# Slots, late mixing and prologue order of an attention and FFN block on one Trainium2 core

## The chip, the cores and the metric

One core of a Trainium2 chip runs the whole program. The metric is the device time of one execution in microseconds (us), the median of several runs. Below, TensorE is also called PE, VectorE DVE, ScalarE ACT, GpSimd POOL and SyncE SP, as in the profile's rows.

## The reference

The input x has 8 batch rows of 512 tokens and 256 channels. The output is `x + attention(layernorm(x)) + ffn(layernorm(x))`, in float32:

```python
xn = _layernorm(x, axis=-1)
q, k, v = xn @ Wq, xn @ Wk, xn @ Wv        # 32 query heads, 8 kv heads of 64
q, k = _rope(q, k)
allowed = (j <= i) & (i - j < 128)          # causal, window of 128
attn = softmax(where(allowed, q k^T / 8, -inf))
a = (attn @ v) @ Wo
h = fwht(xn * SU_ug) / SCALE
g = silu(h @ W_gate.T * (Ws[1024:] * SCALE)) * (h @ W_up.T * (Ws[:1024] * SCALE))
f = fwht(g * SU_dp) / SCALE @ W_down.T * (Ws_dp * SCALE)
```

`fwht` is a normalised Walsh-Hadamard transform, linear, so it can be folded into the weights once: the weights of gate and up are multiplied by the Hadamard matrix and by the signs `SU_ug`, and each of their 2048 output columns has a scale.

## The kernel before, in words

Every large product is done in fp32r with operands split in a high part (an ACT copy, rounded) and a low part (DVE: full minus high). Helper `three` (lines 936 to 940) issues three matmuls, high by high, low by high and high by low, and accumulates them in PSUM. A projection of 128 columns for 512 tokens is 2 x 3 = 6 matmuls of 512 columns.

**A batch row ("row")** has an FFN part and an attention part.

- FFN part (PE lines 1130 to 1147): for 8 hidden tiles j, `hidden("gate", j)`, `hidden("up", j)` and `down(j - 2)`. Before tiles 2 and 4 the two projections of a query group go in between. ACT takes silu of the gate (L614), DVE multiplies by up (L836), ACT and DVE split the product (L643, L697). The values v for token tiles 0 and 1 come last. The part ends when DVE adds the sum to `acc` (L891); this row in the trace marks where one batch row's FFN ends.
- Attention part (PE lines 1161 to 1172): 32 steps (8 kv heads x 4 token tiles), two to a unit, in 17 units u = 0 to 16. In a unit PE does `scores(2u)`, `scores(2u+1)` (L1082), `transposes(2u-2)` (L1096), `fill(2u)`, `transposes(2u-1)`, `fill(2u+1)`, and `values_mixed(u-1)` (L1113, L1125). The last unit has no scores. DVE masks the scores and takes their maximum (L851 or L856, then L858), ACT takes the exponentials (L619), POOL divides by the sum (L504), PE transposes, ACT copies the result out (`t_copy`, L629), POOL masks a copy (L512), PE multiplies by the values. ACT copies the output (`o_copy`, L635) and DVE makes its low part (`o_low`, L697), which also gives the PSUM tile TR free: `transposes` of an even step waits for it (`tr_read`). For token tiles 1 to 3, DVE makes `v_mix` (L898, L899, two copies) and POOL `v_step` (L519) from v.

**Slots.** `fill(n)` issues what is put into slot n by hand: a rope projection of the list `ROPE_SLOTS` (first and second half; DVE's `products`, L741, then POOL's `rotate`, L480 and L482), an output projection of `WO_SLOTS` (12 matmuls of 256 columns; DVE adds it to `acc`, `wo_add`, L768), v for tiles 2 and 3 (slots 1 and 3), or the two transposes of the next row's normalised x (`X_SLOT`, L969; ACT `x_high` L567, DVE `x_low`). All of them go through the two PSUM banks of PROJ in turn, in the order of the list USES: use u waits until use u - 2 has been read (`has_read`, line 942). The last output projections of a row, (7, 0) and (7, 1), are issued within the next row's first two hidden tiles (line 1139).

Each engine's instructions run in the order in which its block lists them; a wait holds everything behind it. SP's block issues nearly all loads, with waits of its own.

**Row 0** also splits the query and output weights (`wq_high`, `wq_low`, `wo_high`, `wo_low`): at the slots of WQ_SPLIT_SLOT and WO_SPLIT_SLOT, ACT and DVE do so at the end of a unit (lines 687 to 691 and 925 to 929). The result is saved to DRAM and loaded by later rows.

**The prologue** folds the gate and up weights. SP loads them in two pieces of 1 MB after x has come (line 358) and broadcasts the column scales over partitions (line 360). PE transposes x, projects k and q, and then multiplies 8 tiles of 512 columns by the Hadamard matrix (L1022, 16 matmuls). For each tile DVE reads the product, scales it by sign and column into `folded` (L796), ACT makes the high part from it (L591), DVE the low part (L697). Then come wq(1), the v weights, and hidden tile 0. POOL rotates k first and then does the three butterfly levels of the down weights (L495, L497), which `down_weights` (L1028) needs.

The few lines that order a unit on DVE:

```python
for u in range(UNITS):
    if u: inverse_sum(2 * u - 1)
    if u >= 2: o_low(b, u - 2)
    if u < UNITS - 1: fold(2 * u); fold(2 * u + 1)
    if u < TT - 1: value_mix(u + 1)
    if u < UNITS - 1: inverse_sum(2 * u)
```

## Time and profile before

| | |
|---|---|
| median of 3 runs | 1334.5 us (1334.47 to 1335.08) |
| profiled execution, its own time | 1334.04 us |
| its span, first to last instruction | 1331.5 us |
| granted TensorE clock, mean | 0.993 of full speed |
| busy: PE, DVE, ACT, POOL | 94%, 70%, 56%, 48% |
| FFN of row 0 ends (L891) | 92.5 us |
| FFN of rows 1 to 7 end | 264.6, 422.2, 579.9, 739.2, 896.9, 1056.2, 1213.9 us |
| HBM read, written | 73.21 MB, 12.58 MB |

From one L891 to the next is one period: the attention of a row and the FFN of the next. The table gives 172.1 us for the first, and 157.6, 157.7, 159.3, 157.7, 159.3 and 157.7 us for the others. The last attention takes from 1213.9 us to the end. In a timeline row the first number is the start, the second the duration, both in us; in square brackets stands the engine's idle time just before, and what ended it.

### The profile page before, as it was taken

The numbers are of one execution on the slowest core, as the hardware profiler recorded it, in microseconds if no ns is written. First come the engines' busy times: TensorE is split into PE (matmuls) and PEld (weight loads), VectorE is DVE, ScalarE is ACT, GpSimd is POOL, SyncE is SP. The second block draws the span as 40 slices with busy tenths as digits, with TensorE's granted clock in tenths as the row PEclk, the third lists the DMA queues.
The fourth block names the chain that finished last, engine by engine and source line by source line (L and its number), as shares of the span: only waits on it lengthen the run. The fifth ranks groups of instructions, "written<-read, shape, count | busy, mean of one in ns | idle before, by whom it ended". The sixth has DMA issues, their size and how long they took to land.

```text
span 1331.5 us, 38038 instructions
## 1 busy us (share of the span) xinstructions
PE 1253.3 (94%) x14568; PEld 1065.0 (80%) x14568; DVE 934.4 (70%) x1672; ACT 744.0 (56%) x2813; POOL 645.1 (48%) x655
## 2 busy tenths in 40 slices
PE   6698989999999999999999999999999999999997
PEld 3586777878888888878888788887888878887886
DVE  5657885488845887467864788548885588745885
ACT  2336664367734676256762667436773467725675
POOL 5315553266532756335652465426554266533563
PEclk9899999999999999999999999999999999999999
DMA  7223352424332442423424144142433244341332
GB/s 246 60 76 112 121 166 78 123 76 138 100 106 63 112 122 88 129 62 105 136 65 143 41 128 137 55 121 75 125 106 104 72 113 117 92 127 46 108 106 63
DMA packets 71570, 138.60 MB, mean 104 GB/s; under 512 B 15328, under 2 KB 29152, under 8 KB 71136
## 3 DMA queue, kind: packets, MB, share of 16 engines
q1 hardware_dynamic: 70400, 135.46, 35.0%
q8 instruction: 117, 1.92, 0.6%
q10 hardware_dynamic: 992, 0.73, 0.2%
q14 instruction: 61, 0.50, 0.1%
HBM read 73.21 MB, written 12.58 MB: 64 GB/s over the span
## 4 chain that ended last, share of the span: by engine, by line
PE 77%; DVE 13%; ACT 6%; issue 3%; DMA 0%; DVEq 0%
PE PROJ L938 14%; PE PROJ L939 14%; PE PROJ L940 14%; PE S L1082 8%; PE TR L1096 8%; PE O L1113 5%; PE O L1125 4%; ACT e_sb L619 4%; PE TR L1113 4%; PE S L938 2%; DVE negmax L858 2%; PE S L939 2%; PE S L940 2%; DVE o_lo L697 2%; DVE S L856 2%
## 5 line engine op out<-in xcount | busy, mean ns | idle before, releaser
L619 ACT ACTIVATE e_sb<-S,negmax 128x128 f32<-128x128 f32 x1024 | 364.2, 382 | 37.6 <-DVE negmax L858 35.1
L504 POOL TENSOR_TENSOR e_sb<-e_sb,rinv 128x512 f32<-128x512 f32 x256 | 264.0, 1040 | 68.6 <-DVE rinv L863 67.7
L512 POOL TENSOR_SCALAR_AFFINE_SELECT p_cur<-pt_sb 128x512 f32<-128x512 f32 x192 | 123.9, 649 | 272.7 <-ACT pt_sb L629 272.7
L629 ACT ACTIVATE pt_sb<-TR 128x512 f32<-128x512 f32 x256 | 154.5, 603 | 161.3 <-PE TR L1096 161.3
L741 DVE TENSOR_TENSOR prod<-PROJ,rope_sb 128x1024 f32<-128x1024 f32 x160 | 193.4, 1210 | 62.3 <-PE PROJ L940 62.3
L619 ACT ACTIVATION_READ_ACCUMULATOR e_sb<-S,negmax 128x1 f32 x1024 | 227.3, 222 | 0.0
L1082 PE MATMUL S<-k_stack,q_stack 64*64 64x64 f32 (+2 forms) x5632 | 183.0, 269 | 1.3 <-ACT e_sb L619 1.3
L858 DVE TENSOR_REDUCE negmax<-S 128x4 f32<-128x512 f32 x256 | 177.1, 692 | 8.9
L1096 PE MATMUL TR<-ident,e_sb 128*128 128x128 f32 x1024 | 159.2, 278 | 24.5 <-DVE o_lo L697 21.4
L1082 PEld LDWEIGHTS S<-k_stack,q_stack 64*64 64x64 f32 x5632 | 163.6, 135 | 8.2 <-ACT e_sb L619 5.3
L480 POOL TENSOR_TENSOR qy<-prod 128x512 f32<-128x512 f32 x64 | 82.3, 1286 | 178.4 <-DVE prod L741 178.3
L1096 PEld LDWEIGHTS TR<-ident,e_sb 128*128 128x128 f32 x1024 | 117.3, 141 | 63.9 <-issue 22.0
L614 ACT ACTIVATE staging_rest<-PROJ 128x512 f32<-128x512 f32 x64 | 38.3, 598 | 230.9 <-PE PROJ L940 230.9
L938 PE MATMUL PROJ<-wo_ring,o_hi 128*128 128x256 f32 x512 | 152.7, 298 | 0.0
L939 PE MATMUL PROJ<-wo_ring,o_hi 128*128 128x256 f32 x512 | 143.0, 279 | 0.0
L940 PE MATMUL PROJ<-wo_ring,o_lo 128*128 128x256 f32 x512 | 142.9, 279 | 0.0
L836 DVE TENSOR_TENSOR p_cur<-PROJ,staging_rest 128x512 f32<-128x512 f32 x64 | 44.3, 692 | 136.9 <-PE PROJ L940 136.2
L851 DVE COPY_PREDICATED S<-diagonal_key,S 128x512 f32<-128x512 int8 x192 | 131.5, 685 | 0.7 <-PE S L1082 0.7
L1113 PE MATMUL O<-pt_sb,v_sb 128*64 128x128 f32 x1024 | 106.4, 286 | 19.2 <-DVE v_mix L899 17.8
L938 PE MATMUL PROJ<-xt_hi,wq_ring 128*128 128x512 f32 x256 | 111.7, 436 | 2.7 <-DVE prod L741 1.9
L938 PE MATMUL PROJ<-xt_hi,wgu_hi 128*128 128x512 f32 x256 | 102.8, 402 | 8.3 <-ACT staging_rest L614 6.6
L697 DVE TENSOR_TENSOR o_lo<-TR,o_hi 128x256 fp32r<-128x256 f32 x128 | 53.4, 417 | 81.6 <-ACT o_hi L635 81.6
(104 smaller groups left out, 2882.4 us busy)
## 6 DMA issues: line engine op xcount, KB each, us to landing
q_stack<-qy SPq DMA_DIRECT2D x512, 64.0 KB, 2.0
wq_ring<-wq_split_d SPq DMA_DIRECT2D x56, 512.0 KB, 4.2
wo_ring<-wo_split_d SPq DMA_DIRECT2D x56, 512.0 KB, 3.8
k_stack<-ky SPq DMA_DIRECT2D x256, 64.0 KB, 2.6
x_in<-x SPq DMA_DIRECT2D x8, 512.0 KB, 4.5
wq_split_d<-wq_ring SPq DMA_DIRECT2D x8, 512.0 KB, 3.3
wo_split_d<-wo_ring SPq DMA_DIRECT2D x8, 512.0 KB, 2.8
out<-acc SPq DMA_DIRECT2D x8, 512.0 KB, 5.0
```

Of the source, the lines that this page charges most:

```text
L504: nc.gpsimd.tensor_tensor(e, e, r, ALU.mult).then_inc(norm_done, 1)
L619: last = nc.scalar.activation(e_sb[:, n % 2, r, :], s_heads(n, 1)[:, r, :], ACT.Exp, bias=negmax[:, n % 2, r:r + 1], accum_out=rowsum[:, n ...
L629: nc.scalar.activation(pt_sb[:, n % 4, :, :], TR[:, :, :], ACT.Copy).then_inc(t_copied, 1)
L741: nc.vector.tensor_tensor(prod[:, 2 * part:2 * part + 2, :], both, rope_sb[:, :, :], ALU.mult).then_inc(prod_done, 1)
L851: nc.vector.copy_predicated(own.rearrange("p r (a k) -> p r a k", a=2), diagonal_key[:, :, :].rearrange("p r (a k) -> p r a k", a=2), diagonal
L858: nc.vector.tensor_reduce(negmax[:, n % 2, :], own, axis=AX.X, op=ALU.max, negate=True).then_inc(max_done, 1)
L938: nc.tensor.matmul(dst, lhs[0], rhs[0], start=first, stop=False)
L939: nc.tensor.matmul(dst, lhs[0], rhs[1], start=False, stop=False)
L940: return nc.tensor.matmul(dst, lhs[1], rhs[0], start=False, stop=last)
L1082: last = nc.tensor.matmul(dst[:, at:at + (blocks - 1) * step + 1:step, :], q_stack[rows, g % 2, slot, i * P + a * HP:i * P + (a + 1) * HP] ...
L1096: last = nc.tensor.transpose(TR[:, r, :], e_sb[:, n % 2, r, :], ident[:, :])
L1113: last = nc.tensor.matmul(O_half[a][odd * D:(odd + 1) * D, s, :, :], v, pt_sb[:, (2 * pair + s) % 4, odd:REP:2, a * HP:(a + 1) * HP], star ...
```

## The change

It alters five things.

1. **Slots.** `ROPE_SLOTS` are moved forward: the second half of query group 4 goes from slot 6 to slot 5 (which was empty), and what follows up to two slots earlier. The x transposes go from slot 25 to slot 22, and their ACT and DVE steps are given places of their own: ACT `x_high(0)` after `t_copy(20)`, `x_high(1)` at the end of unit 11; DVE `x_low(0)` between the two folds of unit 11, `x_low(1)` between those of unit 12. Output projection (6, 1) goes from slot 33 to 32, (7, 0) from the next row to slot 33.
2. **Late mixing.** In every row but the last, `values_mixed` of the last pair moves from the end of unit 16 into the next row, between gate 0 and up 0. In the last unit slot 32 is filled before the first transposes.
3. **v_mix of token tile 3** goes from behind the folds of unit 2 to its beginning, ahead of `o_low`.
4. **Weight splits of row 0**: ACT at the beginning of a unit, DVE between the folds and `inverse_sum`.
5. **Prologue.** The gate and up weights are loaded in four quarters, the first behind x; the wait for x and the broadcast of the column scales go. The scales are a small tile [128, 16], used where gate and up are read: silu has a scale, and DVE's product is a scalar_tensor_tensor. The fold has one DVE pass instead of two: ACT reads PSUM with the sign as scale, DVE makes the low part from PSUM. PE folds quarter 0 before x is transposed, quarter 1 after, 2 and 3 after k and q. POOL does the first butterfly level ahead of rotating k. The Silu table is loaded early. DVE waits for all constants before it inverts the deviation of row 0.

The diff, cut to its core:

```diff
@@ slots
-    ROPE_SLOTS = {("q", 3, 0): (0, 2), ("q", 4, 0): (4, 6), ("k", 1, 0): (8, 10), ("q", 5, 0): (12, 14),
-                  ("q", 6, 0): (16, 18), ("q", 7, 0): (20, 22), ("k", 0, NEXT): (26, 28), ("q", 0, NEXT): (30, 32)}
-    X_SLOT = 24
+    ROPE_SLOTS = {("q", 3, 0): (0, 2), ("q", 4, 0): (4, 5), ("k", 1, 0): (6, 8), ("q", 5, 0): (10, 12),
+                  ("q", 6, 0): (14, 16), ("q", 7, 0): (18, 20), ("k", 0, NEXT): (25, 26), ("q", 0, NEXT): (28, 30)}
+    X_SLOT = 22
     WO_SLOTS = {TT * g + TT + 3 + 2 * part: (g, part) for g in range(NKV - 1) for part in range(2)}
-    WO_SLOTS[X_SLOT] = WO_SLOTS.pop(X_SLOT + 1)
+    WO_SLOTS[24] = WO_SLOTS.pop(25)
+    WO_SLOTS[32] = WO_SLOTS.pop(33)
+    WO_SLOTS[33] = (NKV - 1, 0)
-    WQ_SPLIT_SLOT = {2: 4, 9: 5, 13: 6, 18: 7}
+    WQ_SPLIT_SLOT = {2: 4, 8: 5, 12: 6, 16: 7}
-        if n == X_SLOT + 1 and b + 1 < BATCH:
+        if n == X_SLOT and b + 1 < BATCH:
             found += [("x", b + 1, 0, c) for c in range(CT)]
@@ sync: loads of the prologue
             sp.dma_start(x_in[:, :, :], x[0, :, :].rearrange("(t p) c -> p t c", p=P)).then_inc(x_loaded, 16)
+            load_gate_up(0)
             sp.dma_start(kv_stage[:, 0, :, :], tiles(wk)).then_inc(wk_in, 16)
             load_wq(0, 0)
-            sp.wait_ge(x_loaded, 16)
-            for c in range(CT):
-                sp.dma_start(gu_stage[:, c, :], w_gate_up[c * P:(c + 1) * P, :]).then_inc(gu_in, 16)
-            for n in range(2):
-                sp.dma_start(scale_gu_b[n], scale_gate_up[n:n + 1, :].partition_broadcast(P)
-                              ).then_inc(scales_in, 16)
-            sp.dma_start(scale_d_b[:, :], scale_down.partition_broadcast(P)).then_inc(scales_in, 16)
-            sp.wait_ge(wk_in, 16)
+            load_gate_up(1)
             sp.dma_start(wd_stage[0].rearrange("p (f c) -> p f c", f=FT),
                          w_down.rearrange("(f p) c -> p f c", p=P)).then_inc(wd_in, 16)
+            load_gate_up(2)
+            load_gate_up(3)
+            sp.dma_start(scale_d_b[:, :], scale_down.partition_broadcast(P)).then_inc(scale_d_in, 16)
@@ gpsimd
-            rotate(0, "k", 0)
             pool.wait_ge(wd_in, 16)
             for level in range(3):
...
+                if not level:
+                    rotate(0, "k", 0)
@@ scalar
+            def fold_high(n):
+                k, c = divmod(n, CT)
+                act.wait_ge(fold_ready, n + 1)
+                nc.scalar.activation(wgu_p[0][:, c, k * 512:(k + 1) * 512], S4[:, n % 4, :], ACT.Copy,
+                                     scale=su_in_sb[:, c:c + 1]).then_inc(fold_hi, 1)
             deviation(0)
+            act.wait_ge(ident_in, 16)
+            load_table(ACT.Silu)
             act.wait_ge(wk_in, 16)
             nc.scalar.activation(wk_p[0][:, :, :], kv_stage[:, 0, :, :], ACT.Copy).then_inc(w_hi, 1)
+            act.wait_ge(su_done, 2)
+            fold_high(0)
+            fold_high(1)
             x_high(0, 0)
             x_high(0, 1)
             wq_high(0)
+            for n in range(CT, CT * 4):
+                fold_high(n)
             wq_high(1)
...
                 for u in range(UNITS):
+                    for n in (2 * u, 2 * u + 1):
+                        if not b and n in WQ_SPLIT_SLOT:
+                            wq_high(WQ_SPLIT_SLOT[n])
+                        if not b and n in WO_SPLIT_SLOT:
+                            wo_high(WO_SPLIT_SLOT[n])
                     if u:
                         t_copy(2 * u - 2)
+                    if 2 * u == X_SLOT and b + 1 < BATCH:
+                        x_high(b + 1, 0)
                     if u < UNITS - 1:
                         exps(2 * u)
...
                     if u:
                         o_copy(u - 1)
-                    for n in (2 * u, 2 * u + 1):
-                        if not b and n in WQ_SPLIT_SLOT:
-                            wq_high(WQ_SPLIT_SLOT[n])
-                        if not b and n in WO_SPLIT_SLOT:
-                            wo_high(WO_SPLIT_SLOT[n])
+                    if 2 * u == X_SLOT and b + 1 < BATCH:
+                        x_high(b + 1, 1)
@@ vector
+            def fold_low(n):
+                k, c = divmod(n, CT)
+                dve.wait_ge(fold_hi, n + 1)
+                nc.vector.scalar_tensor_tensor(
+                    out=wgu_p[1][:, c, k * 512:(k + 1) * 512], in0=S4[:, n % 4, :], scalar=su_in_sb[:, c:c + 1],
+                    in1=wgu_p[0][:, c, k * 512:(k + 1) * 512].bitcast(fp32), op0=ALU.mult, op1=ALU.subtract
+                ).then_inc(fold_lo, 1)
             row_stats(0)
+            dve.wait_ge(consts_in, CONSTS * 16)
...
             row_rstd(0)
...
             low(wk_p[1][:, :, :], kv_stage[:, 0, :, :], wk_p[0][:, :, :]).then_inc(w_lo, 1)
+            fold_low(0)
+            fold_low(1)
             for c in range(CT):
                 x_low(0, c)
             wq_low(0)
+            fold_low(2)
             products(0, "k", 0, 0)
             products(0, "k", 0, 1)
+            fold_low(3)
+            fold_low(4)
+            products(0, "q", 0, 0)
+            products(0, "q", 0, 1)
+            for n in range(5, CT * 4):
+                fold_low(n)
             wq_low(1)
...
-                    nc.vector.tensor_tensor(h_sb[j % 2], PROJ[:, bank, :], silu_sb, ALU.mult).then_inc(h_done, 1)
+                    nc.vector.scalar_tensor_tensor(out=h_sb[j % 2], in0=PROJ[:, bank, :],
+                                                   scalar=scale_gu_sb[:, 2 * j + 1:2 * j + 2], in1=silu_sb,
+                                                   op0=ALU.mult, op1=ALU.mult).then_inc(h_done, 1)
...
                     if u:
                         inverse_sum(2 * u - 1)
+                    if u == 2:
+                        value_mix(3)
                     if u >= 2:
                         o_low(b, u - 2)
                     if u < UNITS - 1:
                         fold(2 * u)
+                    for part in range(2):
+                        if 2 * u == X_SLOT + 2 * part and b + 1 < BATCH:
+                            x_low(b + 1, part)
+                    if u < UNITS - 1:
                         fold(2 * u + 1)
-                    if u < TT - 1:
+                    if u < 2:
                         value_mix(u + 1)
+                    for n in (2 * u, 2 * u + 1):
+                        if not b and n in WQ_SPLIT_SLOT:
+                            wq_low(WQ_SPLIT_SLOT[n])
+                        if not b and n in WO_SPLIT_SLOT:
+                            wo_low(WO_SPLIT_SLOT[n])
                     if u < UNITS - 1:
                         inverse_sum(2 * u)
@@ tensor
+            pe.wait_ge(had_in, 16)
+            fold_gate_up(0)
             pe.wait_ge(ident_in, 16)
             for c in range(CT):
                 transposed_x(0, c)
+            fold_gate_up(1)
             pe.wait_ge(w_lo, 1)
             for kind in ("k", "q"):
                 for part in range(2):
                     project(0, kind, 0, part)
+            fold_gate_up(2)
+            fold_gate_up(3)
...
                             hidden(name, j)
-                        if b and not n:
-                            project_out(b - 1, NKV - 1, j)
+                            if b and not j and name == "gate":
+                                values_mixed(b - 1, STEPS // 2 - 1)
+                        if b and j == 1:
+                            project_out(b - 1, NKV - 1, 1)
...
-                    if u:
-                        transposes(2 * u - 2)
-                    fill(2 * u)
+                        if u:
+                            transposes(2 * u - 2)
+                        fill(2 * u)
+                    else:
+                        fill(2 * u)
+                        transposes(2 * u - 2)
...
-                    if u:
-                        values_mixed(u - 1)
+                    if 1 <= u < UNITS - 1 or b == BATCH - 1 and u:
+                        values_mixed(b, u - 1)
```

## Rows read from the trace of the kernel before

**Rows 1.** The page's first part: busy time of each engine.

```profile
PE 1253.3 (94%) x14568; PEld 1065.0 (80%) x14568; DVE 934.4 (70%) x1672; ACT 744.0 (56%) x2813; POOL 645.1 (48%) x655
```

**Rows 2.** Stretches: length, PE, PEld, DVE, ACT, POOL busy, clock, DMA share, GB/s.

```profile
0.00:92.50 92.50, 71.29 (x295) 51.23 (x296) 54.77 (x85) 26.84 (x42) 30.29 (x24) 0.96 0.42 137
...
92.50:264.60 172.10, 155.04 (x1818) 132.69 (x1818) 120.05 (x216) 96.96 (x361) 78.48 (x80) 0.99 0.38 116
...
264.60:422.20 157.60, 152.95 (x1817) 131.16 (x1816) 112.30 (x203) 90.75 (x349) 78.30 (x80) 1.00 0.36 102
...
910.00:920.00 10.00, 7.84 (x120) 6.71 (x113) 8.34 (x16) 5.00 (x22) 7.61 (x8) 0.84 0.48 129
```

**Rows 3.** Timeline of PE: its idle times over 1 us in one middle row.

```profile
440.63 0.44 PE L1113 MATMUL O<-pt_sb,v_sb 128*64 128x128 f32 x4 [2.15 <-DVE v_mix L899]
...
506.69 0.66 PE L969 MATMUL PROJ<-ident,xn 128*128 128x128 f32 x4 [1.06 <-DVE acc L768]
...
529.75 0.63 PE L1096 MATMUL TR<-ident,e_sb 128*128 128x128 f32 x4 [1.05 <-DVE o_lo L697]
```

**Rows 4.** Timeline of PE: the first matmul of gate 1, the second q(1) projection.

```profile
45.00 0.79 PE L938 MATMUL PROJ<-xt_hi,wgu_hi 128*128 128x512 f32 x1 [6.56 <-ACT staging_rest L614]
...
58.34 0.50 PE L938 MATMUL PROJ<-xt_hi,wq_ring 128*128 128x512 f32 x1 [1.90 <-DVE prod L741]
```

**Rows 5.** Timeline of row 0: the longest of PE's idle times behind weight splits.

```profile
108.97 0.63 PE L1096 MATMUL TR<-ident,e_sb 128*128 128x128 f32 x4 [2.63 <-DVE o_lo L697]
```

**Rows 6.** Timeline, prologue: DVE's two passes on a fold tile, ACT's table load, hidden tile 1.

```profile
25.99 0.75 DVE L796 SCALAR_TENSOR_TENSOR e_sb<-S,su_in_sb,p_cur 128x512 f32<-128x512 f32 x1
...
26.66 1.99 DVE L697 TENSOR_TENSOR wgu_lo<-e_sb,wgu_hi 128x512 fp32r<-128x512 f32 x1
...
43.06 1.28 ACT L614 ACT_TABLE_LOAD   x1
...
50.32 0.69 DVE L836 TENSOR_TENSOR p_cur<-PROJ,staging_rest 128x512 f32<-128x512 f32 x1 [4.65 <-PE PROJ L940]
```

**Rows 7.** DMA issues of the first 60 us: KB each, median us to landing.

```profile
kv_stage<-wk SPq DMA_DIRECT2D x1, 512.0 KB, 5.8
```

**Rows 8.** Timeline, prologue: the fold matmuls of PE, a half level of POOL's butterfly.

```profile
19.69 13.89 PE L1022 MATMUL S<-gu_stage,had 128*128 128x512 f32 x32
...
25.42 2.68 POOL L495 TENSOR_TENSOR pt_sb<-v_sb 128x1024 f32<-128x1024 f32 x1
```

**Rows 9.** Chain that ended last, prologue: steps of projection matmuls of PE.

```profile
16.17 0.23 PE PROJ L938
...
47.07 0.43 PE PROJ L939
```

**Rows 10.** Timeline: two `v_mix` copies of row 0; then unit 2 of row 1.

```profile
97.38 0.41 DVE L898 COPY v_mix<-v_sb 64x512 f32<-64x512 f32 x1
...
112.49 1.40 DVE L899 COPY v_mix<-v_sb 64x512 f32<-64x512 f32 x1
...
276.36 0.65 ACT L606 ACTIVATE v_sb<-PROJ 128x512 f32<-128x512 f32 x1
...
277.75 0.42 DVE L697 TENSOR_TENSOR o_lo<-TR,o_hi 128x256 fp32r<-128x256 f32 x1 [1.02 <-ACT o_hi L635]
...
277.92 1.27 POOL L519 TENSOR_TENSOR v_step<-v_sb 128x512 f32<-128x512 f32 x1
...
281.14 0.79 DVE L898 COPY v_mix<-v_sb 64x512 f32<-64x512 f32 x1
```

**Rows 11.** Timeline of row 2, unit 12: scores, fold, slot 24, `t_copy`.

```profile
501.29 1.27 PE L1082 MATMUL S<-k_stack,q_stack 64*64 64x64 f32 x40
...
502.82 0.74 DVE L856 COPY_PREDICATED_SCALAR S<-later_key,masked 128x512 f32 x1
...
503.10 0.36 PE L938 MATMUL PROJ<-wo_ring,o_hi 128*128 128x256 f32 x1
...
503.38 0.60 ACT L629 ACTIVATE pt_sb<-TR 128x512 f32<-128x512 f32 x1 [1.19 <-PE TR L1096]
```

126 lines of the change are left out of this document (47 added, 79 removed).

## The prediction

> **What bounds the kernel now.** I read the busy shares first: PE is busy for 94% of the span, the next engine for 70% [rows 1]. Then the stretches from one end of an FFN to the next [rows 2]: a middle row takes 157.6 us, of which PE is busy 152.95. Row 0's attention with row 1's FFN takes 172.1 us with hardly more PE work (155.04), and the prologue with row 0's FFN has 21.2 us without PE (92.50 - 71.29). So the PE program sets the time, and a change that adds no PE work can win or lose only in PE's idle times and in its clock. Third comes the timeline of PE, and there only the brackets. A middle row has three idle times over 1 us [rows 3]: 2.15 before `values_mixed(1)`, which waits for `v_mix` of tile 3; 1.06 between the two x transposes, the second of which waits for a `wo_add`; 1.05 before the first transposes of unit 16, which has no scores to hide `o_low`. Their sum, 4.26, is nearly all of 157.6 - 152.95. In the prologue the largest are 6.56 and 1.90 us [rows 4]. In row 0 the transposes wait up to 2.63 us for `o_low`, which stands on DVE behind the weight splits [rows 5]; eight idle times of this kind sum to 11.8 us.
>
> The profiled execution took 1334.04 us (span 1331.5), 0.5 below the median of the runs. The sum below is against 1334.04; about 0.5 goes on top for the median.
>
> **Prologue: 14.5 us less.** Gate 1 starts at 45.00 [rows 4] behind this queue: the fold paced by DVE, which takes 0.75 for the first pass and up to 1.99 for the second [rows 6], then wq(1), the v weights, a table load of 1.28 [rows 6], and silu. I walk the new order. Quarter 0 stands second in SP's queue where wk stood; wk was issued at 1.30 and took 5.8 [rows 7]: PE starts at 7.1 instead of 8.6. The fold is 32 matmuls in 13.89 us, 0.43 apart at full clock [rows 8]; a quarter is 8 of them, 3.5 us. PE begins at the lower level of its clock (1.2 GHz), as it did at 45.00, where its projection matmuls ran 0.43 apart for 4.6 us, against 0.23 at 2.4 GHz [rows 9]. So quarter 0 takes 5.8 and ends at 12.9. Transposes 1.1, quarter 1 3.5, k and q 24 x 0.23 = 5.6, quarters 2 and 3 6.9: gate 0 can start at 30.0. DVE follows, since a tile now costs it one pass of 0.75 instead of 0.75 + 1.99. ACT: the last high part 0.6, wq(1) 0.6, the v weights 1.0, silu 0.6, no table load: gate 1 at about 32.9. Up 1 ends at 35.7; in the old trace DVE took it up at 50.32 [rows 6]. That is 14.6 earlier, partly since gate 1 and up 1 run at 2.4 GHz instead of 1.2. Behind it the same chain (down weights, their scaling, q(1)) leads to 58.34 [rows 4]. It needs POOL's butterflies: rotating k waits for k's products (21.5), ends at 24.0, and four half levels of 2.68 [rows 8] to 2.8 end at 35.0. They are covered by 0.7 us only; if k's products come later, the chain moves with them. The wait for all constants ahead of `row_rstd` is hidden by quarter 0: x is wanted at 12.9 only; without that cover it would cost what the constants are late. Bounds: 9 if PE stays at 1.2 GHz through quarter 1 (3.5 more) and POOL is 2 late, 17 if the clock rises early. I take 14.5.
>
> **v_mix(3) at the beginning of unit 2: 10 us less.** The wait of 2.15 [rows 3] goes in all 8 rows, and slot 5 puts a projection of 1.4 us there. What is late next: v of tile 3 is copied by 276.36 + 0.65 = 277.0, `o_low` starts at 277.75 [rows 10]. The two copies would start at 277.05. Where nothing is in the way a copy takes 0.41, with POOL at work 0.79 and 1.40 [rows 10]. POOL is in a tensor_tensor up to 277.92 and then in `v_step` [rows 10]. So the copies end between 277.9 and 279.6, and `o_low`, and behind it the transposes, come 0.1 to 1.7 late. I take 0.9 (the first copy waits for 277.92, the second is free): 2.15 - 0.9 = 1.25, times 8. Bounds 0.4 and 2.1 per row.
>
> The Trainium skill, "SBUF — State Buffer", section "SBUF: two separate sides", says that VectorE in a two-port mode and GpSimd take a shared port pair by an exclusive lock for a whole instruction, and the other blocks fully. The copy of 1.40 agrees. By it `v_step` could take the lock at 277.92 ahead of the second copy; that case is a rival below.
>
> **The x transposes at slot 22: 12.6 us more.** The wait of 1.06 goes: `wo_add(3,1)` is done when the second transpose comes. But both are read on a longer path. Unit 11: PE does scores 1.27, transposes 0.4, x0 and x1 0.4 each, transposes 0.5, and is at slot 23 at +3.15. Slot 23 waits for `x_low(0)`: transposes at +1.42, `t_copy` at +2.09 for 0.60 [rows 11], `x_high` 0.6, `x_low` 0.7: +4.05. That is 0.9 idle, and 0.1 before the transposes. Unit 12: slot 24 waits for `x_low(1)`, which stands behind fold(24). In the trace scores start at 501.29, fold(24) at 502.82 (behind `o_low` and so behind `o_copy`), and PE is at slot 24 at 503.10 [rows 11]. Fold 1.35 and `x_low` 0.7 end at 504.9: 1.8 idle. Together 2.8 for 1.06: 1.8 more, in 7 rows. Bounds 0.5 and 3 per row: nothing covers fold(24), since `o_low` ahead of it waits for PE's own last matmul, so I see no gain here unless DVE runs ahead.
>
> **Row 0's splits: 9 us less.** ACT makes the high part while it would wait for transposes, and DVE's 0.7 comes ahead of `inverse_sum`, in a unit where DVE has about 0.9 idle. Of the 11.8 us, and 0.5 by which the v wait is longer there, I leave 1.2 in unit 2 (three splits at once) and 2.1 in units 6, 8 and 10 (two splits, or one with the normalising of x). Bounds 4 and 12.
>
> **Boundary of rows: 1 us less.** The wait of 1.05 [rows 3] is covered by slot 32; but the second transposes now follow the first at once and wait for `t_copy`, 0.8, and silu(0) stands behind `o_copy(15)`, 0.1. Net 0.15 in 7 rows; between -0.5 and +1 each. The last row gives back up to 1.4 (unit 11 loses a projection that hid its exponentials), I take 1.1; the very end, where one output projection now waits for `o_low`, comes out 0.3 earlier.
>
> **Clock: 2.7 us less.** After the v wait the granted clock fell in 3 of 8 rows (0.84 in [rows 2], to 1.2 GHz for some 3 us), 1.6 us each: 4.8. After waits of about 1 us it never fell. The new 1.8 may bring between none and 3 of 8 back: half, 2.1.
>
> Costed at nothing: the scaled product of the hidden tiles (0.75 as in [rows 6] for 0.69, DVE waits there for PE anyway, 4.65 [rows 6]); the earlier rope slots, each still a unit behind its rotation; SP's queue, where `load_wo(7)` can go at the end of unit 14 and is wanted in unit 16.
>
> **Sum.** -14.5 - 10 + 12.6 - 9 - 1 + 1.1 - 0.3 - 2.7 = -23.8; 1334.04 - 23.8 = 1310.2, and 1310.7 for the median.
>
> **The rivals.**
> - A, x is hidden (0.12). If DVE and ACT run ahead so that slots 23 and 24 find x read, the 12.6 go, 1298; at best the old 1.06 x 7 = 7.4 goes too, 1291. Against it: the order on DVE is written out.
> - B, v_mix is blocked (0.12). `v_step` starts at 277.92 ahead of the second copy and holds it to the end, as the copy of 1.40 was held: the transposes come 1.7 late in each of 8 rows, 0.8 more than summed: 6.4, so 1317. This is what the lock of the Trainium skill's page "SBUF — State Buffer" would do. If the x stalls also bring the clock down in 3 rows, 1320.
> - C, the prologue gives half (0.10). PE's 1.2 GHz lasts through quarter 1, or quarter 0 lands late because 4 MB are queued together: 7 us lost, 1318.
> - D, slower (0.04). Place: slots 23 and 24. Each exponential behind a late fold delays `t_copy` of the odd step, and so `values_mixed`. If both units run at the pace of that chain, 5.5 us are lost per row beyond the sum: 38 more, 1349. It decides above (1334.5 - 1310.7) / 7 = 3.4 per row.
> - E, the moves don't do what they are for (0.08): in the rows each idle time that goes comes back at another place, and only the prologue's 14.5 stay: 1320.
>
> **How the numbers follow.** The forecast has 0.53. The range reaches to A on one side and to B, C and E on the other: 1297 to 1322. Changes under 0.2% (2.7 us) can't be told from none. Faster by more: the forecast, A, B, C and E, 0.95; the same 0.01, D with a smaller price; slower 0.04. The range leaves out D, and the far ends of A and C.
>
> **What would show it.** FFN of row 0 ending near 78 instead of 92.5; fold tiles with one DVE pass of 0.75; no `v_mix` wait over 1 us, but transposes waiting for `o_low` in unit 2; x waits of about 0.9 and 1.8 us in 7 rows, named as `xt_lo`; middle rows of about 157.4 us, and row 0 near 163. If the middle rows fall by more than 1 us, my account of x is wrong; if row 0's FFN ends after 85, that of the prologue.

## The result: 0.8% faster, and the profile after

| | before | after |
|---|---|---|
| median (lowest to highest) | 1334.79 us (1334.47 to 1335.36, 4 runs) | 1323.55 us (1322.25 to 1325.11, 4 runs) |
| profiled execution | 1334.04 us, span 1331.5 | 1322.25 us, span 1320.5 |

The ratio is 0.9918, with a 95% interval of 0.9906 to 0.993: faster by 11.2 us. Forecast were 1310.7 (1297 to 1322), so the sign was right and the time lies above the range.

The page of the changed kernel, its first part (busy time of each engine), answers to [rows 1]:

```profile
PE 1257.2 (95%) x14568; PEld 1063.4 (81%) x14568; DVE 939.3 (71%) x1664; ACT 751.9 (57%) x2814; POOL 647.9 (49%) x655
```

PE's work has not shrunk: its busy time grew by 3.9 us, and its idle time fell by 14.9. The stretches answer to [rows 2] (length, PE, PEld, DVE, ACT and POOL busy, granted clock, DMA share, GB/s):

```profile
0.00:83.40 83.40, 69.25 (x295) 48.92 (x296) 48.05 (x77) 28.02 (x43) 29.80 (x24) 1.00 0.42 140
83.40:244.50 161.10, 155.40 (x1817) 132.54 (x1817) 120.14 (x215) 97.74 (x361) 79.49 (x80) 0.99 0.40 124
244.50:403.50 159.00, 153.94 (x1817) 131.44 (x1817) 114.04 (x203) 91.71 (x349) 78.64 (x80) 1.00 0.34 101
721.40:881.90 160.50, 155.44 (x1817) 132.63 (x1816) 114.13 (x203) 91.76 (x349) 78.68 (x80) 0.99 0.33 100
730.00:740.00 10.00, 8.11 (x92) 6.39 (x91) 9.35 (x15) 6.42 (x30) 8.32 (x8) 0.92 0.35 107
1201.80:1320.50 118.70, 105.94 (x1562) 91.02 (x1560) 88.45 (x163) 75.99 (x323) 66.75 (x71) 0.99 0.29 86
```

Read the lengths against those of before: the first stretch lost 9.1 us (92.5 to 83.4), row 0 lost 11.0 (172.1 to 161.1), the last gained 1.1. A middle row went from 157.6 to 159.0. With the rows in which the clock fell, the six together (244.50 to 1201.80, 957.3 us) are 8.0 longer than before (264.6 to 1213.9, 949.3). So the change is two gains of 20.1 and a loss of 9.1 in the very rows that it was to leave alone or mend. Forecast were -14.5, -8.6, +2.4 without the clock, and -0.5.

Where does a middle row wait now? PE's idle times of over 0.4 us there (start, duration, and in brackets the idle time before it and what ended it) answer to [rows 3]:

```profile
260.23 0.63 PE L1113 MATMUL TR<-ident,e_sb 128*128 128x128 f32 x4 [1.89 <-DVE o_lo L710]
...
322.25 0.39 PE L948 MATMUL PROJ<-wo_ring,o_hi 128*128 128x256 f32 x1 [0.49 <-DVE xt_lo L710]
...
328.63 0.39 PE L948 MATMUL PROJ<-wo_ring,o_hi 128*128 128x256 f32 x1 [1.60 <-DVE xt_lo L710]
...
356.38 0.63 PE L1113 MATMUL TR<-ident,e_sb 128*128 128x128 f32 x4 [0.78 <-ACT pt_sb L640]
```

All three waits of [rows 3] are gone, and four others stand in their place. The wait for `v_mix` has turned into one for `o_low` in unit 2; that for `acc` into two for `xt_lo` in units 11 and 12; that in unit 16 into one of 0.78 for `pt_sb`. Why `o_low` is late is seen on DVE, ACT and POOL of the same unit:

```profile
255.89 2.06 POOL L507 TENSOR_TENSOR e_sb<-e_sb,rinv 128x512 f32<-128x512 f32 x2
...
256.35 0.66 ACT L616 ACTIVATE v_sb<-PROJ 128x512 f32<-128x512 f32 x1
...
257.04 1.19 DVE L905 COPY v_mix<-v_sb 64x512 f32<-64x512 f32 x1 [0.31 <-ACT v_sb L616]
...
257.90 1.44 POOL L522 TENSOR_TENSOR v_step<-v_sb 128x512 f32<-128x512 f32 x1
...
258.24 1.39 DVE L906 COPY v_mix<-v_sb 64x512 f32<-64x512 f32 x1
...
259.66 0.42 DVE L710 TENSOR_TENSOR o_lo<-TR,o_hi 128x256 fp32r<-128x256 f32 x1
```

The first copy ends 0.3 us after POOL's normalising multiplication, the second 0.3 after `v_step`, and each takes about three times the 0.41 of a free one [rows 10]. `o_low` stands right behind them. This is rival B's picture: a lock held for a whole instruction, as the Trainium skill, "SBUF — State Buffer", section "SBUF: two separate sides", has it.

The prologue, PE's idle times, then DVE's instructions behind gate 0:

```profile
7.50 5.60 PE L1024 MATMUL S<-gu_stage,had 128*128 128x512 f32 x8 [7.50 <-DMA gu_stage<-w_gate_up]
13.58 1.64 PE L979 MATMUL PROJ<-ident,xn 128*128 128x128 f32 x8 [0.49 <-DVE xn L737]
22.56 0.50 PE L948 MATMUL PROJ<-xt_hi,wq_ring 128*128 128x512 f32 x1 [1.09 <-DVE prod L754]
39.17 0.50 PE L948 MATMUL PROJ<-xt_hi,wgu_hi 128*128 128x512 f32 x1 [2.19 <-DVE p_cur L841]
49.03 0.50 PE L948 MATMUL PROJ<-xt_hi,wq_ring 128*128 128x512 f32 x1 [1.96 <-DVE prod L754]
```

```profile
33.93 2.30 DVE L713 SCALAR_TENSOR_TENSOR wq_ring<-wq_stage,wq_ring 128x512 fp32r<-128x512 f32 x1
36.16 2.30 DVE L710 TENSOR_TENSOR wv_lo<-kv_stage,wv_hi 128x1024 fp32r<-128x1024 f32 x1
38.38 0.74 DVE L841 SCALAR_TENSOR_TENSOR p_cur<-PROJ,scale_gu_sb,staging_rest 128x512 f32<-128x512 f32 x1
```

Up 1 (39.17) waits 2.19 us for the bank that hidden tile 0 (38.38) gives back, and this one stands behind two weight splits of 2.30 each. In the kernel before, with POOL idle, the same two splits took 0.69 and 1.23:

```profile
42.21 0.69 DVE L700 SCALAR_TENSOR_TENSOR wq_ring<-wq_stage,wq_ring 128x512 fp32r<-128x512 f32 x1
43.07 1.23 DVE L697 TENSOR_TENSOR wv_lo<-kv_stage,wv_hi 128x1024 fp32r<-128x1024 f32 x1 [0.17 <-ACT wv_hi L595]
```

In the changed kernel POOL is at work beside both, in a butterfly up to 35.69 and then in q's rotation. The two are 2.7 us longer than free, more than up 1 waits. The second q(1) projection is at 49.03 instead of 58.34 [rows 4]: those 9.3 us are the stretch's 9.1.

### The profile page after: what moved, and what is told of

Its sections match the earlier page's. It is cut to its first block, busy times and chain, and to the rows that moved or that the text cites. A ratio compares the mean times of both kernels' runs of the same rounds, so it can differ in the third digit from the quotient of the medians.

```text
span 1320.5 us, 38033 instructions
## 1 busy us (share of the span) xinstructions
PE 1257.2 (95%) x14568; PEld 1063.4 (81%) x14568; DVE 939.3 (71%) x1664; ACT 751.9 (57%) x2814; POOL 647.9 (49%) x655
## 4 chain that ended last, share of the span: by engine, by line
PE 84%; DVE 8%; ACT 6%; issue 2%; DMA 1%; ACTq 0%; DVEq 0%
PE PROJ L948 15%; PE PROJ L950 15%; PE PROJ L949 15%; PE S L1099 10%; PE TR L1113 9%; PE O L1130 5%; PE O L1142 4%; PE TR L1130 4%; ACT e_sb L630 3%; PE S L948 2%; PE S L950 2%; PE S L949 2%; ACT pt_sb L640 1%; DVE S L863 1%; DVE v_mix L906 1%
## 5 line engine op out<-in xcount | busy, mean ns | idle before, releaser
L1099 PE MATMUL S<-k_stack,q_stack 64*64 64x64 f32 (+2 forms) x5632 | 179.8, 266 | 1.7 <-ACT e_sb L630 1.7
L948 PE MATMUL PROJ<-wo_ring,o_hi 128*128 128x256 f32 x512 | 155.0, 303 | 16.0 <-DVE xt_lo L710 14.6
L1099 PEld LDWEIGHTS S<-k_stack,q_stack 64*64 64x64 f32 x5632 | 160.2, 133 | 8.6 <-ACT e_sb L630 5.7
L624 ACT ACTIVATE staging_rest<-PROJ,scale_gu_sb 128x512 f32<-128x512 f32 x64 | 44.2, 690 | 209.3 <-PE PROJ L950 205.4
L949 PE MATMUL PROJ<-wo_ring,o_hi 128*128 128x256 f32 x512 | 144.6, 282 | 0.0
L841 DVE SCALAR_TENSOR_TENSOR p_cur<-PROJ,scale_gu_sb,staging_rest 128x512 f32<-128x512 f32 x64 | 48.1, 751 | 130.4 <-PE PROJ L950 130.4
L948 PEld LDWEIGHTS PROJ<-wo_ring,o_hi 128*128 128x128 f32 x512 | 97.7, 191 | 21.2 <-DVE xt_lo L710 18.0
L781 DVE TENSOR_TENSOR acc<-PROJ,acc 128x512 f32<-128x512 f32 x128 | 87.5, 684 | 31.1 <-PE PROJ L950 31.0
```

Source lines behind the costliest of these rows:

```text
L948: nc.tensor.matmul(dst, lhs[0], rhs[0], start=first, stop=False)
L949: nc.tensor.matmul(dst, lhs[0], rhs[1], start=False, stop=False)
L1099: last = nc.tensor.matmul(dst[:, at:at + (blocks - 1) * step + 1:step, :], q_stack[rows, g % 2, slot, i * P + a * HP:i * P + (a + 1) * HP] ...
```

## The experiments

Each is one edit to the changed kernel, unless said otherwise. All ratios are to the kernel before. The first eight take the stretches apart; the last four test the mechanisms and put the repairs together.

### v_mix of tile 3 behind the folds again

```diff
-                    if u == 2:
-                        value_mix(3)
...
-                    if u < 2:
+                    if u < TT - 1:
                         value_mix(u + 1)
```

> The changed kernel, but the v_mix copies of tile 3 stand behind the folds of unit 2 again; slot 5 keeps its projection. Theory 1 (the place ahead of o_low costs, since POOL's v_step holds the copies for 1.19 and 1.39 us instead of 0.41): the wait of 1.89 us before the transposes of unit 2 falls under 0.2, a wait of about 0.7 (2.15 less the projection of 1.49) comes at values_mixed(1), middle rows go from 159.0 to 157.8 us, the whole is about 9 us faster than the changed kernel. Rival (DVE has too much in unit 2 with two rope products, wherever the copies stand): the waits of unit 2 still sum to 1.5 or more, middle rows stay at 158.6 or more. On the clock: if its falls follow idle times near 2 us, no row shows one, and 3 x 1.6 us go besides; if they come anyway, two or three rows of 8 still take 1.6 us longer.

Measured: 1313.97 us (1312.39 to 1316.32), ratio 0.9845 (0.9831 to 0.986). The stretch of row 1, and what is left of the waits of its unit 2:

```profile
245.42:403.32 157.90, 153.91 (x1817) 131.42 (x1816) 112.83 (x203) 91.54 (x349) 78.58 (x80) 1.00 0.35 102
```

```profile
263.87 0.44 PE L1128 MATMUL O<-pt_sb,v_sb 128*64 128x128 f32 x4 [0.83 <-DVE v_mix L906]
```

Putting the move back makes the kernel 9.6 us faster than the change. In rows 1 to 7 the copies at the old place now cost 0.83 of waiting (1.35 in row 0), not the 2.15 of [rows 3]: the change puts a projection of 1.4 us at slot 5, ahead of these matmuls, and 2.15 - 1.4 is 0.75. So my gain for this move was measured against a wait that another part of the change had already covered but for 0.83, and the move put 1.89 in its place. A middle row is 1.1 shorter where neither execution lost clock in it. In this execution the clock fell in no row, but it did in the first stretch, which ends at 84.76. Rows 0 and 6 gained only 0.5 (although the fall of the clock in row 0 is gone) and 0.1: in both, PE now also waits 1.09 and 0.70 for POOL's masked copy (`p_cur`), which it did not in the changed kernel.

### x_low(1) ahead of fold(24)

```diff
+                    if 2 * u == X_SLOT + 2 and b + 1 < BATCH:
+                        x_low(b + 1, 1)
                     if u < UNITS - 1:
                         fold(2 * u)
...
```

> The changed kernel, but x_low(1) stands ahead of fold(24) on DVE instead of behind it. Theory 2 (slot 24 waits 1.60 us because fold(24), 1.35 us, is in the chain from PE's last matmul to x_low): the wait falls to about 0.3, middle rows go from 159.0 to 157.7, the whole is 9 us faster than the changed kernel. Rival (the exponentials, now 0.7 later, are the next bound): the wait comes back before scores or transposes of units 12 and 13, rows fall by less than 0.5.

Measured: 1314.57 us (1311.16 to 1316.46), ratio 0.9846 (0.9829 to 0.9863). The same two waits of units 11 and 12:

```profile
322.47 0.38 PE L949 MATMUL PROJ<-wo_ring,o_hi 128*128 128x256 f32 x1 [0.49 <-DVE xt_lo L710]
...
327.56 0.39 PE L949 MATMUL PROJ<-wo_ring,o_hi 128*128 128x256 f32 x1 [0.31 <-DVE xt_lo L710]
```

1.60 has become 0.31. Rows in which the clock held take 157.7 (402.38 to 560.04) instead of 159.0 (row 6: 158.0 for 159.3); 1.3 to 1.4 in 7 rows is the 9 us. The fold that goes behind costs nothing that shows. This is the term that I had priced at 1.8, and its cause is the order on DVE, as the prediction had it.

### The prologue alone

The changed kernel with units, slots, splits and mixing as they were before.

> The kernel before with the new prologue, the quarters, the scales at use and the early Silu table alone; slots, late mixing, v_mix, x and splits are the old ones. Theory 3 (the parts add up): row 0's FFN ends at 83.4 as in the changed kernel (92.5 before), the following stretches take 172.1 and 157.7 as before, in all 1325.7 us. Rival (the scaled operands at use slow the FFN of each row by some 0.2 us, as the late stretch of the changed kernel's rows may show): middle rows of 157.9, 1327. If the clock falls less or more often without the change of rows, 1.6 us per row.

Measured: 1330.35 us (1329.27 to 1332.14, 7 runs), ratio 0.9969 (0.9958 to 0.9981). The first FFN ends at 85.12 (granted clock 0.66 from 40 to 45, behind the waits of up 1; behind the same wait it did not fall in the changed kernel, where the stretch ends at 83.40), row 0 takes 170.75, and an undisturbed middle row 158.0 instead of 157.6. So the prologue keeps 7.4 of its us at the end of the first stretch and only about 4 at the end of the kernel: the rows are longer by 0.3 to 0.4 although no unit was touched. The run on the scale tile below takes that up.

### Hidden tile 0 ahead of the last splits

```diff
+                if not b:
+                    wq_high(1)
+                    act.wait_ge(wv_in, 16)
+                    nc.scalar.activation(wv_p[0][:, :, :], kv_stage[:, 1, :, :], ACT.Copy).then_inc(w_hi, 1)
                 silu(1)
...
                     hidden(j)
+                    if not b and not j:
+                        wq_low(1)
+                        dve.wait_ge(w_hi, 2)
+                        low(wv_p[1][:, :, :], kv_stage[:, 1, :, :], wv_p[0][:, :, :]).then_inc(w_lo, 1)
```

> The changed kernel, but silu(0) stands ahead of the high parts of wq(1) and the v weights on ACT, and hidden tile 0 ahead of their low parts on DVE. Theory 4 (the prologue fell 5.4 us short since low passes from SBUF to SBUF took 2.30 us each under POOL and held hidden tile 0): the wait of 2.19 before up 1 goes, row 0's FFN ends near 80.5 instead of 83.4, 2.9 us faster. Rival (the low passes now hold hidden tile 1 or the scaling of the down weights just as long): row 0's FFN ends at 82.5 or later.

Measured: 1324.42 us (1321.26 to 1327.03), ratio 0.9921 (0.9899 to 0.9943): no gain. DVE and then PE:

```profile
35.51 0.75 DVE L839 SCALAR_TENSOR_TENSOR p_cur<-PROJ,scale_gu_sb,staging_rest 128x512 f32<-128x512 f32 x1 [1.40 <-PE PROJ L952]
36.18 1.42 DVE L714 SCALAR_TENSOR_TENSOR wq_ring<-wq_stage,wq_ring 128x512 fp32r<-128x512 f32 x1
37.53 2.30 DVE L711 TENSOR_TENSOR wv_lo<-kv_stage,wv_hi 128x1024 fp32r<-128x1024 f32 x1
39.74 0.74 DVE L839 SCALAR_TENSOR_TENSOR p_cur<-PROJ,scale_gu_sb,staging_rest 128x512 f32<-128x512 f32 x1
```

```profile
47.81 0.50 PE L950 MATMUL PROJ<-xt_hi,wq_ring 128*128 128x512 f32 x1 [3.35 <-DVE prod L755]
```

Hidden tile 0 comes 2.9 us earlier (35.51 for 38.38) and the wait of up 1 is gone, but `wv_lo` now holds hidden tile 1, and behind it the down weights. The wait moved from up 1 to the q(1) projection (3.35 for 1.96), which starts only 1.2 earlier; from 45 to 55 the granted clock is 0.83, and the stretch ends at 83.81. The rival was right: the splits have to leave this queue.

### The last pair mixed in unit 16 again

```diff
-                            if b and not j and name == "gate":
-                                values_mixed(b - 1, STEPS // 2 - 1)
...
-                    if 1 <= u < UNITS - 1 or b == BATCH - 1 and u:
+                    if u:
                         values_mixed(b, u - 1)
```

> The changed kernel, but the last pair of every row is mixed at the end of unit 16 again, behind output projection (7, 0). Theory 5 (late mixing gains nothing: the span from unit 16 to the first q projection of the next FFN takes 13.69 us against 13.53 before, once a q projection of 1.49 is taken off): middle rows change by less than 0.3 us, the whole by less than 2.5. Rival (the mixing in the FFN hides a wait of its own: t_copy and mask of step 31 must be done before values_mixed(15), and gate 0 covers them): a wait of 0.5 to 1 before values_mixed(15) in each row, 4 to 8 us slower than the changed kernel.

Measured: 1326.12 us (1321.81 to 1327.91), ratio 0.993 (0.991 to 0.9951). By the times it can't be told from the change. Its stretch of row 1, and the wait of unit 16 beside the mixing:

```profile
246.14:404.95 158.81, 153.77 (x1817) 131.57 (x1816) 113.96 (x203) 91.65 (x349) 78.52 (x80) 1.00 0.35 101
```

```profile
357.92 0.63 PE L1113 MATMUL TR<-ident,e_sb 128*128 128x128 f32 x4 [0.78 <-ACT pt_sb L640]
359.91 0.44 PE L1130 MATMUL O<-pt_sb,v_sb 128*64 128x128 f32 x4
```

The mixing (359.91) waits for nothing at its old place, and the 0.78 ahead of it is the one that the change has too. So it is not the late mixing that took the 1.05 of [rows 3] away. What is left of the change at this place is that slot 32 is filled first, with an output projection; a run that undoes this alone was not made. Rows are 0.05 to 0.2 shorter without the late mixing.

### The splits alone

The kernel before, with only the weight splits of row 0 moved as in the change.

> The kernel before with one part of the change alone: row 0's weight splits at the beginning of a unit on ACT and ahead of inverse_sum on DVE. Theory 6 (the waits of transposes behind splits, 11.8 us in sum, were ACT's high part behind o_copy): the first stretch takes 163 to 165 us instead of 172.1, the later ones 157.7 as before, in all 7 to 9 us faster than before. Rival (the gain of row 0 in the changed kernel came from the slots moved forward, DVE has no room for the low parts): the stretch stays above 169.

Measured: 1328.06 us (1323.96 to 1332.47, 10 runs), ratio 0.9951 (0.9934 to 0.9967). Row 0 takes 164.8 us, 7.3 less than the 172.1 of [rows 2], although the clock fell for longer in it: the mean granted clock from 110 to 120 us is 0.66, and 0.83 in the kernel before. At 1.6 us for one such fall, the splits themselves gain about 8.9.

```profile
93.61:258.42 164.81, 156.09 (x1817) 133.73 (x1816) 119.94 (x216) 96.72 (x361) 79.16 (x80) 0.98 0.41 121
```

Its two longest waits are 2.69 for `v_mix` and one that I had not seen behind the old ones:

```profile
169.22 0.63 PE L1096 MATMUL TR<-ident,e_sb 128*128 128x128 f32 x4 [2.16 <-ACT pt_sb L629]
```

The change has neither of them in row 0, but waits 2.53 for `o_low` and 1.60 for `xt_lo` there. Its row 0 is another 3.7 shorter (161.1): PE's idle times of over 0.25 us sum to 5.4 for 8.4, and the clock fell once less. The ten runs lie between 1323.96 and 1332.47, with mean granted clocks of 0.992 down to 0.986, so the 6.1 us by which the medians differ hold clock as well.

### The v weights' split later

The split of the v weights and wq(1) out of the way of hidden tiles 0 and 1: wq(1) behind silu(0) and hidden tile 0, the v weights in FFN stage 2.

```diff
...
                     if not b and n in WQ_SPLIT_IN_FFN:
                         wq_low(WQ_SPLIT_IN_FFN[n])
+                    if not b and n == 2:
+                        dve.wait_ge(w_hi, 2)
+                        low(wv_p[1][:, :, :], kv_stage[:, 1, :, :], wv_p[0][:, :, :]).then_inc(w_lo, 1)
...
```

> The changed kernel, but silu(0) and hidden tile 0 come first, wq(1)'s split behind them, and the split of the v weights only behind hidden tile 5. Theory 7 (in the run with hidden tile 0 first the low part of the v weights, 2.30 us under POOL, held hidden tile 1 to 39.74): hidden tile 1 is read at about 38.2, the second q(1) projection starts at 46.5 instead of 49.03, row 0's FFN ends near 81. Rival (the chain is then bound by POOL's butterfly and the down weights): the second q(1) projection at 48 or later, row 0's FFN within 0.5 of 83.4.

Measured: 1322.16 us (1315.82 to 1322.45), ratio 0.9894 (0.987 to 0.9919). The first stretch ends at 80.93:

```profile
0.00:80.93 80.93, 68.74 (x295) 49.07 (x296) 46.22 (x78) 28.14 (x43) 28.82 (x24) 1.00 0.44 144
```

```profile
46.54 0.50 PE L952 MATMUL PROJ<-xt_hi,wq_ring 128*128 128x512 f32 x1 [1.94 <-DVE prod L756]
```

2.5 us earlier at both places (49.03, 83.40). In the whole time little of it shows, since in this execution the clock fell in five of eight rows, and in three in that of the change. The run of 1315.82 had a mean granted clock of 1.000, the three near 1322 had 0.993 or 0.994.

### The tile of scales allocated last

```diff
-        scale_gu_sb = sb("scale_gu_sb", [P, 2 * FT])
...
         o_p = [sb(f"o_{s}", [P, REP // 2, T], f32r) for s in ("hi", "lo")]
+        scale_gu_sb = sb("scale_gu_sb", [P, 2 * FT])
```

> The changed kernel, but the tile of the column scales, 64 bytes per partition, is the last one allocated, so that all others lie at their old addresses. Theory 8 (the output projections take 303, 282 and 282 ns a matmul instead of 298, 279 and 279 in every kernel with the tile in front, since the tiles behind it are shifted): 298, 279 and 279 ns again, middle rows 158.7 instead of 159.0, 2 to 3 us in all. Rival (the scaled operands of silu and the product slow the FFN): the means stay, rows of 159.0.

Measured: 1322.3 us (1316.41 to 1326.36), ratio 0.9917 (0.9889 to 0.9944). Every row is 0.3 shorter (158.65 to 158.7). Groups by line, the matmuls of the output projection (count | busy, mean ns): first the changed kernel, then this one.

```profile
L949 PE MATMUL PROJ<-wo_ring,o_hi 128*128 128x256 f32 x512 | 144.6, 282 | 0.0
L950 PE MATMUL PROJ<-wo_ring,o_lo 128*128 128x256 f32 x512 | 144.4, 282 | 0.0
```

```profile
L950 PE MATMUL PROJ<-wo_ring,o_lo 128*128 128x256 f32 x512 | 142.9, 279 | 0.0
L949 PE MATMUL PROJ<-wo_ring,o_hi 128*128 128x256 f32 x512 | 142.9, 279 | 0.0
```

The same matmuls take 279 ns where the 64 bytes per partition of the new tile stand behind all other tiles, and 282 where they stand ahead. So the edit's only effect on the rows is where the tiles lie; through which part of the memory that works no run here shows. The times of this kernel spread over 10 us, and the clock goes with them: 1316.41, 1319.47, 1325.14 and 1326.36 us at mean granted clocks of 0.999, 0.997, 0.992 and 0.991. In the profiled execution, the fastest, it fell in no row behind row 0.

### v_step behind v_mix

This tests the lock by itself. `v_mix` stays where the change put it; only POOL's `v_step` of the same tile waits.

```diff
                 def value_step(i):
+                    if i == TT - 1:
+                        pool.wait_ge(v_mixed, b * (TT - 1) + i)
```

> The changed kernel; v_mix of tile 3 stays where the change put it, and GpSimd's v_step of tile 3 waits until it is made. Theory (v_step, which started at 257.90 ahead of the second copy, held that copy for 1.39): the first copy stays near 1.2 beside the normalising multiplication, the second takes 0.41, o_low comes 1.0 earlier, and the wait of the transposes in unit 2 falls from 1.9 to about 0.9; v_step ends some 0.7 later, unseen. Rows 158.0 instead of 159.0, time about 1315. Rival: the copies are slow for another reason (the tile, the PSUM access of PE or ACT): the second one stays near 1.4, the wait near 1.9, and the time at 1322.

Measured: 1313.77 us (1313.58 to 1313.94), ratio 0.9846 (0.9829 to 0.9862). DVE and POOL in unit 2 of row 1, then PE:

```profile
256.73 1.19 DVE L907 COPY v_mix<-v_sb 64x512 f32<-64x512 f32 x1 [0.31 <-ACT v_sb L618]
257.93 0.42 DVE L908 COPY v_mix<-v_sb 64x512 f32<-64x512 f32 x1
258.38 0.42 DVE L712 TENSOR_TENSOR o_lo<-TR,o_hi 128x256 fp32r<-128x256 f32 x1
...
258.43 1.28 POOL L524 TENSOR_TENSOR v_step<-v_sb 128x512 f32<-128x512 f32 x1 [0.80 <-DVE v_mix L908]
```

```profile
258.95 0.63 PE L1115 MATMUL TR<-ident,e_sb 128*128 128x128 f32 x4 [0.92 <-DVE o_lo L712]
```

The second copy fell from 1.39 to 0.42 and the wait from 1.89 to 0.92, the very value that I had summed for the case without the lock. Five of the rows 1 to 6 take 158.0 to 158.3. `v_step` itself, 0.8 later in its row, delays nobody that shows in them, but row 6 takes 159.7: PE waits 1.20 there for POOL's masked copy (`p_cur`), which it did not in the changed kernel. In row 0 the wait stayed at 2.52: there the second copy, 1.18 long, lies beside POOL's normalising multiplication and not beside `v_step`. So the lock of `v_step` is worth 0.97 in seven rows, 6.8 of the 9.8 us. The rest is mostly clock, which fell in no row here (only in the first stretch, 84.67 for 83.40) and in three in the execution of the change.

### Four repairs together, and two variants

The four: v_mix(3) behind the folds, x_low(1) ahead of fold(24), the v weights later, the tile of scales last.

> The changed kernel with four of the edits already tried alone: v_mix of tile 3 behind the two folds, x_low(1) ahead of fold(24), the v weights split in the FFN of row 0, the tile of scales allocated last. If the four gains are independent they add up: a middle row of 159.0 loses 1.1 + 1.4 + 0.3 and takes 156.2 us, FFN of row 0 ends near 81, and the time is 1322.3 - 9.6 - 9.2 - 2.5 - 2.1 = 1299 us. Rival: where one wait goes the next on the same chain takes its place (v_mix's and x's waits share DVE), so that the rows stay above 157 and the time above 1304.

Measured: 1298.6 us (1297.76 to 1300.01), ratio 0.9733 (0.9719 to 0.9748). Row 1:

```profile
240.80:397.14 156.34, 153.64 (x1817) 130.95 (x1816) 112.85 (x203) 91.39 (x349) 78.58 (x80) 1.00 0.36 103
```

The gains add up: 156.3 against 156.2 expected (157.2 and 157.4 in rows 3 and 6), and the time to 0.4 us. Only the first stretch ends at 82.39 instead of 81; the granted clock was 0.69 from 45 to 50, behind the wait of 1.94 at the q(1) projection. This kernel is 25 us faster than the change and 35.6 faster than the one before.

> The four edits together, and besides them the last pair mixed in unit 16 again, as in the kernel before. Alone that edit gained 0.1 to 0.2 us per row (158.85 against 159.0). If that holds beside the others, rows take 156.1 and the time is within 0.2% of the four together. Rival: with the other waits gone the late mixing is worth what it hides (the wait of 1.05 before the transposes of unit 16), rows take up to 157.2 and the time is 5 to 7 us more.

Measured: 1298.76 us (1297.73 to 1299.92), ratio 0.9734 (0.9719 to 0.9748). Row 1 takes 156.33 us: the late mixing is worth nothing here, and what its undoing gained alone (0.05 to 0.2 per row) does not show beside the others.

> The four edits together, but v_mix of tile 3 between fold(4) and fold(5), where before it was behind both. If what is left there (a wait of 0.83 on the second copy) is only the time at which VectorE comes to it, it starts 1.35 us earlier, the 0.83 goes and each of 8 rows gains up to 0.8: about 1293. Rival: fold(5) and behind it the exponentials of step 5 come 0.8 to 1.4 later and the transposes of unit 3 wait for them: no gain, or up to 0.5 us per row lost (1299 to 1303).

Measured: 1299.42 us (1299.22 to 1301.12), ratio 0.9741 (0.9727 to 0.9756). The wait for `v_mix` is down to 0.20, but the fold behind it delays the exponentials, and two new waits come up:

```profile
256.13 0.44 PE L1135 MATMUL O<-pt_sb,v_sb 128*64 128x128 f32 x4 [0.20 <-DVE v_mix L910]
258.92 0.88 PE L1104 MATMUL S<-k_stack,q_stack 64*64 64x128 f32 x24 [0.45 <-ACT e_sb L627]
260.19 0.63 PE L1118 MATMUL TR<-ident,e_sb 128*128 128x128 f32 x4 [0.39 <-DVE o_lo L712]
```

Rows take 156.8 us, most of them 0.5 more: the rival again, at the upper end of its price. By the rows, behind both folds is the best of the three places tried; by the times (1299.42 for 1298.6, intervals that overlap) it can't be told from the place between the folds.

## Why the prediction was wrong

The sum was -23.8, the span fell by 11.0. By stretch, forecast and measured: prologue -14.5 and -9.1; row 0 -8.6 and -11.0; six middle rows +2.4 and +8.0; last stretch -0.5 and +1.1; clock -2.7 and, contained in the rows, 0. The misses are 5.4 - 2.4 + 5.6 + 1.6 + 2.7 = 12.9.

**v_mix(3), "10 us less": the step that failed.** The two bounds were stated (`o_low` late by 0.1 to 1.7), the row for the lock was there (a copy of 1.40), and I took 0.9 because the second copy would be free. `v_step` took the pair at 257.90, 0.3 before the first copy had ended, and unit 2 waits 1.89. With `v_step` held back the wait was 0.92, my 0.9, so for rows 1 to 7 the mechanism is shown by taking it away. In a middle row unit 2, less the projection of 1.49 that now stands in it, is 0.4 us shorter than before, not 1.25. That is rival B, at 0.12. It was worse than a mis-sized gain: the place behind the folds is 1.1 better per row. I had compared the new place with the old trace, not with the old place in the new order, where only 0.83 was left: my own text had the projection of 1.4 us at slot 5 and drew nothing from it.

**x at slot 22, "12.6 us more": right in kind, a little high.** Slot 23 waited 0.49 instead of 0.9, slot 24 1.60 instead of 1.8; units 11 and 12 cost 1.3 more per row, 9 us in 7 rows. Moving one instruction, `x_low(1)`, took 1.3 of it back. Rival A (x hidden) was wrong.

**Boundary, "0.15 less per row": 0.16 more.** The wait of 0.78 for `t_copy` came as forecast; silu and the late mixing did not repay it.

**My own sum for a middle row did not agree with my text.** -1.25 + 1.8 - 0.15 is +0.4, so a middle row is 158.0; "about 157.4" stood in the last part. Measured 159.0. Of the 1.0 between, 0.85 is unit 2 and some 0.3 each are the boundary and the pace of the output projection, less 0.5 of the x term.

**A term that was missing: 0.3 us per row for a tile of 64 bytes per partition.** Costed at nothing with the scales' use; 2.4 us in eight rows. It looked like noise until the run with the tile at the end.

**Row 0's splits, "9 us less": 7.3 alone,** with one more fall of the clock in it, so about 8.9: right. In company row 0 lost 11.0 although it has the bad v_mix and x terms too; 1.3 of that came with the prologue alone, where row 0 took 170.75 and its `v_mix` wait was 1.12 instead of 2.69. The 2.1 that I had left for units 6, 8 and 10 did not come, and the 2.16 that appears with the splits alone is gone in the new order of units; which of its moves takes it away was not tried.

**Prologue, "14.5 less": 9.1.** Gate 0 starts at 31.94 for 30.0: the transposes took 1.64 for 1.1 and waited 0.49, the first q projection waited 1.09 for k's `prod`, which stood on DVE behind a split of wq(0) of 2.74 (17.98). Then up 1 waits 2.19, which my walk did not contain: I counted ACT's splits ahead of silu (32.9) and left out DVE's, 4.6 us ahead of hidden tile 0. I counted ACT's queue and not that of the engine beside it. And the lengths are the lock's again: 2.74, 2.30 and 2.30 beside POOL, where the kernel before took 0.68, 0.69 and 1.23 for the same splits with POOL idle. (Moved behind hidden tile 0, wq(1)'s took 1.39 to 1.42, still beside POOL.) No run held POOL back beside a split, so for the splits this is read from the durations and not shown. Moving the last two gave 2.5 back. What was right: PE at 7.5 for 7.1, quarter 0 in 5.6 for 5.8, one DVE pass per tile.

**The last stretch, "0.5 less": 1.1 more.** 0.85 of the miss is `v_mix` again. PE also stands idle for 1.34 us before the last output projection (1314.71), a wait that the kernel before did not have and that the profile puts down to no other engine; my sum had this place 0.3 earlier.

**Clock, "2.7 less": none.** Behind waits of 1.9 (2.53 in row 0) it fell in 3 of 8 rows, as behind 2.15 before. I had 1.8 at half the old chance, and by my v_mix term no such wait in unit 2 at all.

**The range.** Its end of 1322 was 1.6 short. It took in B (6.4 more) or a prologue 7 short, not both; both came, the second at 5.4 and for other reasons than C names. Rival E's 1320 is near the time, but not for its reason: row 0 did gain 11 us, and the middle rows lost 8.

## What to carry to other kernels

Price a moved instruction against the order that the whole change makes, not against the old trace: the wait that it is to remove may already be gone, and here the move itself cost 9.6 us. Where VectorE copies or splits from SBUF to SBUF beside GpSimd, take the locked duration (here 1.9 to 4 times the free one) as the likely one, write down what stands behind it on its queue, and hold GpSimd's instruction back if it is not urgent. When several small terms of the same sign depend on one mechanism, widen the range by their sum.
